# Edge passes of a three-layer graph network: units of two edge tiles by one node block in place of single visits

## The reference, cut to what matters

```python
logits = leaky_relu(a_src[src] + a_dst[dst], 0.2)     # layer "gat", 4 heads
alpha = segment_softmax(logits, dst, n)
x1 = segment_sum(h[src] * alpha[:, :, None], dst, n)
logits2 = sum(q[dst] * k[src], -1) * scale            # layer "attn", a dot product of 256 channels
out = segment_sum(v[src] * softmax2[:, None], dst, n)
alpha = leaky_relu(sum(xs[src]*a_s[etype]) + sum(xd[dst]*a_d[etype]))   # layer "typed", 8 heads
out = segment_sum(xs[src] * (softmax3 * edge_weight), dst, n)
```

## Time and profile before

| | |
|---|---|
| median of 3 runs | 5034.81 us (5025.68 to 5041.2) |
| span of the profiled execution | 4992.2 us |
| median less this span (launch and end of the program) | 42.6 us |
| DVE, PE, POOL, ACT busy share of the span | 62%, 68%, 53%, 35% |
| pass gat, from first to last instruction of its visits | about 205 to 1535 us |
| pass attn | about 1768 to 3027 us |
| pass typed | about 3262 to 4604 us |
| packets moved by transfers | 554.64 MB, 111 GB/s |

### The profile page before, as it was taken

The page is one execution under the profiler, slowest core; times in us unless marked ns, Lnnn a source line. Parts: engine busy times, 40 slices in busy tenths (PEclk is TensorE's granted clock), DMA queues, the critical chain, the costliest instruction groups (busy, mean ns, idle before and its releaser), DMA issues. The chain is left out here.

```text
span 4992.2 us, 80536 instructions
## 1 busy us (share of the span) xinstructions
PE 3385.8 (68%) x15489; PEld 2315.7 (46%) x15489; DVE 3110.9 (62%) x10883; ACT 1739.5 (35%) x5661; POOL 2633.7 (53%) x2962
## 2 busy tenths in 40 slices
PE   6366665666677467777777778556666666666999
PEld 4244443444445344444444445334444444433998
DVE  6355555655567555666666667656666666667886
ACT  3333333333335444545455555311121221121332
POOL 3555555555540345555555543555555555553787
PEclk8666677776769788888888889767777777677999
DMA  4444444444433433333333334534433333332221
GB/s 144 134 127 122 125 121 122 127 123 126 122 97 90 129 94 105 107 106 107 103 108 108 110 86 150 182 106 112 112 108 110 111 108 108 109 107 81 72 73 53
DMA packets 286529, 554.64 MB, mean 111 GB/s; under 512 B 83599, under 2 KB 180941, under 8 KB 286126
## 3 DMA queue, kind: packets, MB, share of 16 engines
q0 software_dynamic: 115872, 326.30, 23.8%
q10 hardware_dynamic: 97688, 160.93, 10.6%
q1 hardware_dynamic: 72566, 63.01, 4.5%
HBM read 473.68 MB, written 76.32 MB: 110 GB/s over the span
## 5 line engine op out<-in xcount | busy, mean ns | idle before, releaser
L483 PE MATMUL psum<-big,onehots_or_distances 128*128 128x264 f32 (+2 forms) x4992 | 2151.6, 541 | 1058.1 <-DVE acc L654 486.6
L483 PEld LDWEIGHTS psum<-big,onehots_or_distances 128*128 128x128 f32 x4992 | 1025.5, 250 | 1419.8 <-issue 1274.7
L654 DVE TENSOR_TENSOR acc<-acc,psum 128x264 f32 (+2 forms) x2496 | 1046.1, 419 | 773.7 <-DMA acc<-in_edges_dram,acc 237.2
L267 POOL DMA_INDIRECT big<-table_attn,src_by_edge x782 | 739.8, 946 | 764.5 <-SPq L260 352.2
L267 POOL DMA_INDIRECT big<-table_typed,src_by_edge x782 | 740.3, 947 | 618.7 <-SPq L260 380.8
L267 POOL DMA_INDIRECT big<-table_gat,src_by_edge x782 | 739.2, 945 | 608.5 <-SPq L260 379.1
L373 ACT ACTIVATE onehots_or_distances<-psum 128x512 f32<-128x512 f32 x416 | 248.1, 596 | 1665.6 <-DMA joins<-visit_joins 524.3
L632 DVE TENSOR_TENSOR big<-big,psum 128x256 f32<-128x256 f32 x1664 | 669.1, 407 | 91.6 <-issue 58.7
L426 PE MATMUL psum<-big,onehot_t 128*128 x2496 | 490.5, 311 | 228.7 <-issue 138.8
L508 DVE SCALAR_TENSOR_TENSOR dot_products<-psum,big 128x258 f32<-128x258 f32 x832 | 348.1, 419 | 449.0 <-PE psum L426 228.0
L344 ACT ACTIVATE onehots_or_distances<-iota,tables 128x128 f32<-128x128 f32 x832 | 330.3, 397 | 669.1 <-DVE acc L654 428.5
(11 more groups left out here) (280 smaller groups left out, 4192.3 us busy)
## 6 DMA issues: line engine op xcount, KB each, us to landing
onehot_t<-onehots ACTq DMA_DIRECT2D x68, 512.0 KB
big<-visit_positions ACTq DMA_DIRECT2D x52, 512.0 KB
onehots<-big ACTq DMA_DIRECT2D x36, 512.0 KB
big<-onehots ACTq DMA_DIRECT2D x36, 512.0 KB
big<-in_x_dram SPq DMA_DIRECT2D x98, 128.0 KB, 2.8
big<-table_gat,src_by_edge POOLq DMA_INDIRECT x782
big<-table_attn,src_by_edge POOLq DMA_INDIRECT x782
big<-table_typed,src_by_edge POOLq DMA_INDIRECT x782
```

Of the source, the lines that this page charges most:

```text
L267: pool.indirect_dma_start(X[:, t % RING, :], None, ph.table, bass.IndirectOffsetOnAxis(ap=m.src[:, t:t + 1], axis=0)).then_inc(S[f"rows{t ...
L483: nc.tensor.matmul(sum_ps(v), onehot_at(v), rows, start=True, stop=True).then_inc(S["summed"], 1)
L654: nc.vector.tensor_tensor(row, row, sum_ps(v), ALU.add).then_inc(S["added"], 1)
```

## The change

Visits are ordered in pairs. A **unit** is two neighbouring tiles (256 edges) against one node block; 391 pairs of tiles and 49 blocks make at most 439 units, 440 with padding, which is 880 visits in 55 batches of 16. Both visits of a unit belong to the same block, so PE sums them into one PSUM bank (the second matmul accumulates), `summed`, `added` and `scaled` count units, DVE scales both tiles in one instruction of 512 elements and adds one sum a unit. gat keeps 4 banks, which are now 8 visits; typed and attn have 3 banks, 6 visits. DVE adds a unit two units behind in gat and one unit behind in the others (`behind`). attn's fourth sum bank goes to `expand`, and ACT's `distance` waits for PE's sum and no longer for DVE's add. The ring's places are read by pairs, so a batch's register loads fetch 8 numbers where they fetched 16.

The second part moves the chain of a batch in gat and typed: `copy_tails`, `expand`, the logits, the scans and `shift` stand four visits sooner (`CHAIN_AHEAD`), `weigh` one visit sooner.

```diff
-VISITS = NT + NB - 1
+VISITS = 2 * (NT // 2 + NB - 1)
+PAIRS = G // 2
+CHAIN_AHEAD = 4
-    SB = 3 if ph.typed else 4
-    sum_banks = (0, 1, 2, 7) if ph.dot else range(SB)
-    exp_banks = (3, 4, 5)
+    SB = 4 if ph.name == "gat" else 3
+    behind = SB - 2
+    exp_banks = (3, 4, 5, 7)
...
+    def twins_at(place, lo, hi):
+        return ph.twins[:, bass.ds(place, 1), :, lo:hi].rearrange("p t a w -> p (t a) w")
...
-                nc.scalar.activation(tails_at(k)[:, g, :], X[:, bass.ds(slots[g], 1), D:D + T].rearrange("p a w -> p (a w)"), ACT.Copy).then_inc(S["tails"], 1)
+                nc.scalar.activation(tails_at(k)[:, g:g + 2, :], twins_at(places[g // 2], D, D + T), ACT.Copy).then_inc(S["tails"], 1)
...
-                if v >= SB + 1:
-                    act.wait_ge(S["added"], v - SB)
+                if v >= 5 and v % 2:
+                    act.wait_ge(S["summed"], (v - 3) // 2)
...
-            weigh_at = G - 1 if ph.dot else G - 2
+            weigh_at = G - 1 if ph.dot else G - 3
...
+            def main(v):
+                w = v // 2
+                if not ph.dot and v % 4 == 0:
+                    pe.wait_ge(S["onehots"], v // 4 + 1)
+                if ph.dot:
+                    pe.wait_ge(S["onehot"], v + 1)
+                elif v % 2 == 0:
+                    pe.wait_ge(S["scaled"], w + 1)
+                if v % 2 == 0 and w >= SB:
+                    pe.wait_ge(S["added"], w + 1 - SB)
+                last = nc.tensor.matmul(sum_ps(w), onehot_at(v), rows, start=(v % 2 == 0), stop=(v % 2 == 1))
+                if v % 2:
+                    last.then_inc(S["summed"], 1)
...
-                row = tile_at(slots[g], D).rearrange("p (h c) -> p h c", h=H)
-                nc.vector.tensor_tensor(Y[:, v % YR, 0:D].rearrange("p (h c) -> p h c", h=H), row, spread(row_weights[:, g, :], D // H), ALU.mult).then_inc(S["scaled"], 1)
+                rows = twins_at(places[g // 2], 0, D).rearrange("p a (h c) -> p a h c", h=H)
+                nc.vector.tensor_tensor(Y[:, at:at + 2, 0:D].rearrange("p a (h c) -> p a h c", h=H), rows,
+                                        row_weights[:, g:g + 2, :].unsqueeze(3).to_broadcast([P, 2, H, D // H]), ALU.mult).then_inc(S["scaled"], 1)
...
-                (c + 3, 0, scan_ahead), (c + 3, 1, scan_back), (c + 4, 0, ends), (c + 4, 1, turn_ends), (c + 5, 0, run_scans), (c + 5, 1, from_others),
-                (c + 11, 0, shift)])
+                (6, 1, scan_ahead), (7, 1, scan_back), (8, 1, ends), (8, 1, turn_ends), (9, 1, run_scans), (9, 1, from_others),
+                (15, 1, shift)])
...
-                if v >= 2:
-                    add(v - 2, last_blk if v % G == 1 and v < VISIT_END else blks[(v - 2) % G])
+                if v % 2 and w >= behind:
+                    add(w - behind, last_blk if begins else blks[(w - behind) % PAIRS])
```

More of the change, by code:

```diff
@@ L247, in batch_at, with chain_at @@
             return k if 0 <= k < NBATCH else None, g
+        def chain_at(v):
+            return batch_at(v if ph.dot else v + CHAIN_AHEAD)
         @block.sync
@@ L392, in _ @@
                         transposed_onehot(v // G + 3)
-                u = v + 2 * G - 1
-                if not ph.dot and 0 <= u < VISIT_END:
+                u = v + 2 * G - 1 + CHAIN_AHEAD
+                if not ph.dot and 0 <= u < VISIT_END and u % 2 == 0:
                     if u % G == 0:
-                        slots = needs = ()
-                        slots, needs = slots_of(ACT_ENGINE, u, G), needs_of(ACT_ENGINE, u // G)
-                    copy_tails(u)
+                        places = needs = ()
+                        places, needs = places_of(ACT_ENGINE, u // 2, PAIRS), needs_of(ACT_ENGINE, u // G)
+                    copy_tails(u // 2)
             if ph.name == "gat":
@@ L475, in _ @@
-                    pe.wait_ge(S["onehot" if ph.dot else "scaled"], v + 1)
-                    if not ph.dot and v % G == 0:
-                        pe.wait_ge(S["denominators"], v // G + 1)
-                    if v >= SB and (not ph.dot or v == VISIT_END - 1):
-                        pe.wait_ge(S["added"], v + 1 - SB)
                     if ph.dot and v % 4 == 0:
-                        slots = slots_of(PE_ENGINE, v, 4)
-                    rows = tile_at(slots[v % 4], ph.WS) if ph.dot else Y[:, v % YR, :]
@@ L483, in _ @@
-                    nc.tensor.matmul(sum_ps(v), onehot_at(v), rows, start=True, stop=True).then_inc(S["summed"], 1)
+                        places = places_of(PE_ENGINE, v // 2, 2)
+                    main(v)
                 if not ph.dot and v % 4 == 0 and 0 <= v + 4 < VISIT_END:
                     turn_onehots((v + 4) // 4)
-                k, g = batch_at(v)
+                k, g = chain_at(v)
                 if k is not None:
@@ L636, in rescale @@
                 if k:
[L637 removed]
+                    dve.wait_ge(S["added"], k * PAIRS)
                 if ph.dot:
@@ L653, in add @@
                 row = m.acc[:, bass.ds(blk * WA, ph.WS)]
-                nc.vector.tensor_tensor(row, row, sum_ps(v), ALU.add).then_inc(S["added"], 1)
+                nc.vector.tensor_tensor(row, row, sum_ps(w), ALU.add).then_inc(S["added"], 1)
             c = ph.masked_at
-            summing = {"gat": [(0, 0, source_logits), (0, 1, middle_part), (1, 0, low_part), (1, 1, leaky)],
+            summing = {"gat": [(0, 1, source_logits), (1, 1, middle_part), (2, 1, low_part), (3, 1, leaky)],
                        "attn": [],
-                       "typed": [(0, 0, source_logits), (0, 1, middle_part), (1, 0, low_part), (1, 1, type_one), (2, 0, leaky)]}[ph.name]
@@ L691, in _ @@
+                if begins:
+                    last_blk, blks = (blks[PAIRS - 1] if k else None), blocks_of(k)
+                if v % 2 and w >= behind:
+                    add(w - behind, last_blk if begins else blks[(w - behind) % PAIRS])
                 for at, place, part in parts:
-                    if k is not None and (at, place) == (g, 1):
-                        part(k)
-                if v >= 0 and v % G == 1 and v < VISIT_END:
-                    rescale(v // G, blks[0])
+                    if b is not None and (at, place) == (g, 1):
+                        part(b)
@@ L698 @@
+                if begins:
+                    rescale(k, blks[0])
 class Space:
@@ L1129, in _ @@
                 node(next(step))
[L1130 to L1132 removed]
+            dve.wait_ge(S["last_dst"], 32 * sum(c * P < NT for c in range(VC)))
+            nc.vector.tensor_scalar(last_blk, last_dst, 7, None, ALU.arith_shift_right)
+            c_.step(nc.vector.tensor_scalar(numbers, numbers, 1, None, ALU.bitwise_or))
+            c_.step(nc.vector.tensor_copy(odd, numbers))
+            nc.vector.tensor_tensor(first_half, odd, v_idx, ALU.subtract)
+            c_.step(nc.vector.scalar_tensor_tensor(v_end, last_blk, 2.0, odd, ALU.mult, ALU.add))
             for c in range(VC):
```

177 lines of the change are left out of this document (95 added, 82 removed).

## The result

The changed kernel takes **5000.6 us**, median of 6 runs (4993.7 to 5020.5), against 5038.0 of the kernel before beside it: a ratio of 0.9928, interval 0.9904 to 0.9952. 4717 were forecast. The sign was right and the size was not: 37 us came where 318 were expected. The profiled run took 5002.75 us over a span of 5000.8, so little lies outside the span; before's traced execution was simply some 40 us quicker than the timed ones. The two traced spans are 8.6 us apart the other way, so traces of the two kernels are compared here with some 40 us of doubt.

The account below looks back on a forecast made before the run. It took visits in flight while a tally is late as the bound: gat 230 us less, attn 9, typed 84, 5 us added, so -318: span 4674, plus 42.6 gives 4717 us, range 4380 to 5060.

Parts of the forecast that it names:

- Slack for late tallies: More visits in flight while PE's results are late cut gat 0.73 to 0.45, typed 0.69 to 0.58, attn 0.60 to 0.52.
- the extra: Time a visit that comes with gathers, beyond work: 0.73 us in gat, 0.60 in attn, 0.69 in typed before the change.
- the sum: Work plus extra, times 880 visits: gat 1100 us, attn 1250, typed 1258; with 5 us more, 318 less in all.
- Work: Time a visit without the extra: gat 0.89 to 0.80 us, attn 0.95 to 0.90, typed 0.95 to 0.85.
- The wide scaling: DVE's one scaling of 512 elements in place of two of 0.407 us was taken to cost 0.69 us.
- attn and typed: Forecast change of these two passes: attn 9 us less, typed 84 us less.
- The signs: Checks for being right: gat's adds under 2.6 us a pair, add waits nearly gone, POOL's place waits under 900 us.
- the first sign of being wrong: PE's or ACT's waits for one-hots or copies grow by what the waits for adds lose.
- The 42.6 us: Excess of the median 5034.8 us over the profiled span 4992.2, added to the forecast span.
- The first: Turning and copying one-hots stops as long as adds did; pace stays, 48 more visits cost 227 us: 5262 us, chance 0.12.
- The second: The extra stays a fixed sum a pass, 611, 498 and 578 us; only work falls: 5040 us, chance 0.18.
- The third: Slack hides all of the extra, POOL's gathers bound each pass at some 965 us: 4004 us, chance 0.10.

Follow-up runs that it names:

- run 1: Changed kernel, gat and typed: second PSUM bank for turned one-hots, turned four visits sooner, softmax weights moved to SBUF; 4874.6 us, 0.9702.
- run 5: On top of run 1, DVE reads the chain's turned logits and maxima later after PE's turn in gat and typed; 4884.7 us, 0.9706.
- run 6: Changed kernel, attn alone: one-hot made in the place of its distances, ring of eight visits instead of four; 4988.4 us, 0.9916.
- run 10: Changed kernel, one-hots turned four visits sooner, weights left in PSUM, gat's second bank taken from the sums; 4960.8 us, 0.9834.
- run 9: Changed kernel with only the softmax weights of gat and typed moved from PSUM to SBUF; 4901.6 us, 0.9726.
- run 17: Changed kernel, POOL clears 192 columns and waits after each gather past the first 44 of a pass; ratio 0.9138.
- run 16: Kernel before, POOL clears 256 columns and waits after each gather; 4655.5 us.
- run 13: Changed kernel, POOL clears 256 columns and waits after each gather, weights in PSUM; 4630.0 us, one run.
- run 18: Changed kernel, POOL clears 256 columns and waits after each gather past the first 44 of a pass; 4644.1 us.
- run 4: Changed kernel with each gather replaced by a transfer of 128 consecutive table rows on SyncE's own queue; 3402.6 us.
- run 7: Changed kernel, POOL issues the next four gathers only when the last four have landed; 5425.3 us, one run.
- run 8: Changed kernel, gathers after the first 44 of a pass bring 256 bytes a row instead of about 1050; 5016.3 us, one run.
- run 15: Changed kernel, POOL clears 128 columns and waits after each gather, weights in PSUM; time not in the text.
- run 2: Changed kernel gathering only the first 44 tiles of each pass, later visits using stale rows; 3483.0 us.
- run 3: Kernel before, gathering only the first 44 tiles of each pass, later visits using stale rows; 3883.9 us.

## Why the prediction failed

**The step that failed** is "Slack for late tallies", the term that took the extra from 0.73 to 0.45 us in gat, and the sentence it stands on, that the kernel is bound by how many visits may be in flight while a tally is late. Runs 1, 5, 6 and 10 gave that slack at three more places, and apart from the weights in SBUF it brought 40 us by the medians (run 10 against the changed kernel, 0.9834 against 0.9928), or 27 with the weights in SBUF on both sides (run 1 against run 9, 0.9702 against 0.9726, which their intervals don't part). Measured by passes with and without gathers, the extra did not fall but grew: gat 1330 - 876 = 454 us before and 1326 - 694 = 632 after; attn 270 and 359; typed 395 and 525. In gat that is 0.55 us a visit before and 0.72 after, where the sum had 0.73 falling to 0.45. The work gave 409 us in the three passes, and the wait took 397 back.

**What the runs showed in its place.** PE's results are held while POOL issues gathers 1.25 us apart. In the middle of gat in the changed kernel, nine in ten of the results that are on time during a run of gathers fall in its first 4 us, and hardly one after 8; of the late ones told in the pauses, nine in ten come 1.5 to 3 us after the run's end. By the same count none of ACT's and DVE's own results is over 1 us late there. So PE's loops stop, the ring fills, POOL pauses, the results come, places come free, and POOL starts again. A pass is 782 gathers at 1.70, 1.61 and 1.72 us, pauses included, before, and at 1.70, 1.63 and 1.68 after, whatever PE and DVE could do. Paced to 1.50 or 1.55, POOL hardly pauses, the clock granted in gat rises from 0.72 to 0.75 in run 17, and all passes end near POOL's own time. There little is left of the change. With a pause of 256 columns after every gather the kernel before takes 4655.5 us (run 16) and the changed one 4630.0 (run 13, one run); with the pause past the first 44 the changed one takes 4644.1 (run 18). The kernel before was not run with 192 columns, so what the change is worth at the best pace found is open.

**Point by point.** *Work*: 0.80, 0.90, 0.85 a visit were forecast, 694/880 = 0.79, 1.04 and 0.90 measured without gathers. But the kernel before has 1.05, 1.19 and 1.14 there, not the 0.89, 0.95 and 0.95 of its last stretches. Those do not run the same instructions, as the prediction has it: the earlier trace rows has 98 of PE for 36 visits in gat, 2.7 a visit, where the pass has 3496/832 = 4.2, since the work done ahead for later visits is over. In attn 13 dot products stand there beside 38 adds (2990 to 3026 us):

```profile
L508 DVE SCALAR_TENSOR_TENSOR dot_products<-psum,big 128x258 f32<-128x258 f32 x13 | 5.4, 418 | 1.3 <-PE psum L426 1.1
```

So the work saved was undervalued, 77 us in my sum and 409 measured, and the extra before was overvalued. *The wide scaling*, 0.69 us:

```profile
L657 DVE TENSOR_TENSOR big<-big,psum 128x512 f32<-128x512 f32 x880 | 596.5, 678 | 207.0 <-ACT psum L347 171.3 <-issue 27.6
```

0.678 us, right. *attn and typed*: -9 and -84 forecast, +18 and -26 by the traces; gat -230 and -4. *The signs*: PE's waits for adds fell to 15 us and gat's last stretch fell to 0.71 us a visit, as forecast. The add of a visit pair came every 800/258 = 3.10 us in gat's middle, not under 2.6, POOL waited 1134 us for places, not under 900, and the first sign of being wrong came: PE's waits for copies grew where those for adds went. *The 42.6 us* outside the span were a misreading, as said above.

**The rivals.** The first, that the loop of turned one-hots takes over, is what the waits show: 833 us of PE and its loads for copies, and 1.55 us a visit in gat's middle, over the 1.53 at which it was to decide. But its 5262 us did not come, and to loosen that loop alone gave 40 us, so its price was wrong: the same stall shows wherever PE's result is next needed. The second, that the extra belongs to the gathers, was nearest in time (5040, give or take 60) and in kind; wrong in it is the fixed sum, since the extra took up what the work left. The third put POOL's floor at 1.25 us a gather, 4004 us; at that pace the results are held.

**The Trainium skill's rule** that transfers never contend with a compute engine ("SBUF — State Buffer", "Who interferes with whom") was set against the traces too soon: run 4 agrees with it, 227 GB/s and no late result. It did speak against my reading, in that slack need not shorten such a wait. It names no case in which PE waits while POOL makes gathers, and the table above has one.

**Open** stays what holds PE's results while gathers come faster than about 1.5 us each, and why PE's alone. That it is a queue behind POOL fits runs 7, 8 and 15 to 18, but no run shows the place; scattered addresses are not excluded, and the gain of run 9 is not explained.

## What to carry

A wait that moves from one consumer to the next when slack is given may be caused upstream of all of them: leave the producer out once, as in runs 2 to 4, before counting on slack. Work and wait did not add here: price what a change saves with the suspected cause removed and with it in place. A stretch without the suspect is a fair measure of the work only if it has the same instructions a visit: count them. And an engine that is busy 53% of the span, with its idle time put down to a full ring, may still be what sets the pace, when its bursts hold up those who empty the ring; try a slower, even pace.

## What was unexpected of the hardware

Gathers issued 1.25 us apart hold back PE's results for the length of the run, 10 us in the timeline above, while as many rows by SyncE's queue hold none. The limit is narrow: half the results in gat are late at 1.45 us, a quarter at 1.50 and a twenty-fifth at 1.55 (run 18; 16% in run 13). Clearing 192 columns after each gather past the first 44, 273 ns each, is worth 8% of the changed kernel's time (0.9138 against 0.9928).
